# Four DiT-style layers on one core: preparing the keys of batch 2 between the row maxima of batch 0

## The reference

```python
q = (xq @ Wq + bq).reshape(B, Lq, nh, dh)
kv = (xkv @ Wkv + bkv).reshape(B, Lkv, 2, nh, dh)
scores = jnp.einsum('bqhd,bkhd->bhqk', q, k) / jnp.sqrt(jnp.float32(dh))
attn = jax.nn.softmax(scores, axis=-1)
out = jnp.einsum('bhqk,bkhd->bqhd', attn, v).reshape(B, Lq, H)
return x_q + (out @ Wp + bp)
```

## Time and profile before

| what | value |
|---|---|
| runs, us | 1910.01 (median), 1893.63, 1923.51 |
| profiled execution, us | 1909.95 |
| its span, us | 1908.1 |
| mean granted clock of PE | 0.893 of 2.4 GHz |
| PE busy | 1617.0 us, 85% of the span |
| DVE busy | 1151.9 us, 60% |
| ACT busy | 1002.8 us, 53% |
| POOL busy | 677.6 us, 36% |

### The profile page before, as it was taken

How to read it: one execution, slowest core, us unless ns; L and a number is a source line. 1 busy time by engine, 2 the same in 40 slices (tenths; PEclk the granted TensorE clock), 3 DMA queues, 4 the chain that set the end, 5 groups by cost and what they waited for, 6 DMA issues and landing times.

```text
span 1908.1 us, 54306 instructions
## 1 busy us (share of the span) xinstructions
PE 1617.0 (85%) x20495; PEld 1025.1 (54%) x20495; DVE 1151.9 (60%) x2289; ACT 1002.8 (53%) x1911; POOL 677.6 (36%) x899
## 2 busy tenths in 40 slices
PE   3788878599899998796699999987785899999986
PEld 3365544356566665343366666654342466666664
DVE  5354524377677775354577777771454776777752
ACT  1243423257677776142277777763242476777761
POOL 7000043436666644136166666510232122222200
PEclk9799989779999998697699999996796798999987
DMA  7022203244444432004345544430005444444310
GB/s 188 17 82 64 64 1 81 49 100 124 115 128 130 126 103 77 1 1 113 66 116 137 132 134 127 112 92 1 1 2 119 99 124 126 128 126 131 100 42 10
DMA packets 180074, 166.34 MB, mean 87 GB/s; under 512 B 69087, under 2 KB 169634, under 8 KB 179938
## 3 DMA queue, kind: packets, MB, share of 16 engines
q1 hardware_dynamic: 178354, 163.36, 33.3%
q10 hardware_dynamic: 1008, 1.05, 0.2%
q0 software_dynamic: 576, 0.02, 0.0%
HBM read 114.46 MB, written 40.08 MB: 81 GB/s over the span
## 4 chain that ended last, share of the span: by engine, by line
PE 63%; DVE 11%; ACT 10%; issue 7%; DMA 4%; SPq 3%; POOL 1%; ACTq 0%; DVEq 0%; POOLq 0%
PE PS L1155 11%; PE PS L1050 8%; PE PS L1181 7%; PE PS L1044 7%; PE PS L891 6%; PE PS L1129 5%; PE PS L1039 3%; PE PS L970 3%; SPq L426 2%; PE PS L1255 2%; DVE mx L1553 2%; ACT q_parts L824 2%; PE PS L988 2%; DMA k_dram<-k_lo 2%; ACT v_sb L758 2%
## 5 line engine op out<-in xcount | busy, mean ns | idle before, releaser
L1553 DVE TENSOR_REDUCE mx<-PS 112x1 f32<-112x500 f32 x1152 | 716.2, 673 | 246.9 <-PE PS L1129 242.4
L824 ACT ACTIVATE q_parts<-PS 125x448 f32<-125x448 f32 x1152 | 562.2, 544 | 111.9 <-PE PS L1181 108.4
L573 POOL CAST k_hi<-k_full 128x500 f16<-128x500 f32 x144 | 87.7, 609 | 645.5 <-issue 328.0
L608 POOL TENSOR_SCALAR cx<-cx,norm_b 125x128 f32<-125x128 f32 x384 | 304.8, 808 | 26.4 <-issue 19.3
L1129 PE MATMUL PS<-k_st,q_mx 50*112 50x500 f16 x1152 | 262.5, 403 | 45.4 <-issue 27.5
L1181 PEld LDWEIGHTS PS<-q_st,k_st 50*125 50x125 f16 x4608 | 185.5, 139 | 213.5 <-ACT q_parts L824 147.3
L1181 PE MATMUL PS<-q_st,k_st 50*125 50x112 f16 x4608 | 262.0, 235 | 40.1 <-ACT q_parts L824 22.8
L1155 PE MATMUL PS<-q_parts,v_sb 125*18 125x112 f32 x9216 | 292.8, 271 | 0.0
L1155 PEld LDWEIGHTS PS<-q_parts,v_sb 125*18 125x18 f32 x9216 | 219.4, 101 | 51.9 <-issue 43.8
L575 POOL TENSOR_TENSOR k_lo<-k_full,k_hi 128x500 f16<-128x500 f32 x144 | 164.1, 1139 | 21.1 <-POOL k_hi L573 3.5
L758 ACT ACTIVATE v_sb<-PS 125x512 f32<-125x512 f32 x144 | 87.0, 604 | 107.7 <-PE PS L1050 107.6
(11 more groups left out here) (267 smaller groups left out, 2090.9 us busy)
## 6 DMA issues: line engine op xcount, KB each, us to landing
k_st<-k_dram SPq DMA_DIRECT2D x864, 62.5 KB, 2.2
cx<-in_ctx SPq DMA_DIRECT2D x56, 672.0 KB
k_dram<-k_hi SPq DMA_DIRECT2D x144, 125.0 KB, 1.8
k_dram<-k_lo SPq DMA_DIRECT2D x144, 125.0 KB, 1.9
v_sb<-in_ctx SPq DMA_DIRECT2D x8, 672.0 KB
q_mx<-q_all SPq DMA_DIRECT2D x48, 99.8 KB
q_st<-q_all SPq DMA_DIRECT2D x48, 99.8 KB
cx<-in_ctx SPq DMA_DIRECT2D x56, 78.0 KB
```

What stands on the lines that cost most here:

```text
L608: last = pool.tensor_scalar(cx[:, p, c, :], cx[:, p, c, :], norm_b[:, p, 0, c:c + 1], norm_b[:, p, 1, c:c + 1], ALU.subtract, ALU.mult)
L824: act.activation(probs[:, c % RING, u * HR:(u + 1) * HR], PS[0:KC, (2 * c + u) % SC_RING, 0:HR], ACT.Exp).then_inc(sem("exp_done"), 1)
L1553: dve.tensor_reduce(mx[:, r, t:t + 1], PS[0:PW, MX_BANK + u % MX_RING, 0:TK], AX.X, ALU.max)\
```

## The change

In batch 0 alone of each cross layer, seven pieces of preparation move out of its attention into `first`. PE does V2 of batch 1 after unit 2 of the row maxima, T0, T1, T2 of batch 2 after units 5, 8, 11, and K0, K1, K2 after units 14, 17, 20. ACT does the copies in the same order, before it writes the shift rows of batch 0. V0 and V1 of batch 2 stay in steps 9 and 10 of the attention. GpSimd splits the keys of batch 2 at the end of `first`, now ahead of `normalise` of batch 3. SyncE issues the three `k_out` of batch 2 at the end of `first`, ahead of `q_scores(1)`, `q_max(2)` and `load(4)`. In the attention of batch 0 it only issues two `k_in`, and the third stays in the attention of batch 1. All other batches keep their order.

```diff
--- before.py
+++ after.py
@@ -57,6 +57,9 @@
 SLOT_MISC = {0: (True, 8), 1: (False, 0), 2: (False, 1), 3: (False, 2), 4: (False, 3), 6: (False, 4),
              8: (False, 5), 9: (False, 6), 10: (False, 7)}
 
+FIRST_MISC = {2: (1, 8), 5: (2, 0), 8: (2, 1), 11: (2, 2), 14: (2, 3), 17: (2, 4), 20: (2, 5)}
+FIRST_SLOT_MISC = {9: (False, 6), 10: (False, 7)}
+
 MAXES = [2, 2, 2, 2, 2, 2, 2, 3, 2, 3, 2, 0]
 JOIN_BANK = MX_BANK + 1
 PAIRS = B // 2
@@ -267,6 +270,9 @@
             for b in range(B - 4, B):
                 body(*[at(b + k) if b + k < B else None for k in range(4)])
 
+        def slot_misc(batch):
+            return FIRST_SLOT_MISC if isinstance(batch[0], int) and batch[0] == 0 else SLOT_MISC
+
         def ge_ahead(eng, *waits):
 
 
@@ -478,6 +484,8 @@
                     q_scores((0, 0, 0))
                     q_max((1, 0, 1))
                     stack_q(1, "q_stacked")
+                    for t in range(NT):
+                        k_out((2, 1, 0), t)
 
                 def attend(batch, following, behind, third):
                     b, i, p = batch
@@ -490,11 +498,15 @@
                         q_max(behind)
                         if not (isinstance(b, int) and b + 4 >= B):
                             load((b + 4, i + 2, p))
-                        k_out(behind, 0)
-                        k_in(behind, 0)
-                        k_out(behind, 1)
-                        k_in(behind, 1)
-                        k_out(behind, 2)
+                        if start:
+                            k_in(behind, 0)
+                            k_in(behind, 1)
+                        else:
+                            k_out(behind, 0)
+                            k_in(behind, 0)
+                            k_out(behind, 1)
+                            k_in(behind, 1)
+                            k_out(behind, 2)
 
                 pipeline(sp, first, attend)
 
@@ -623,7 +635,7 @@
                     if third and cr["norm"] is not None:
                         copies(third)
                         normalise(third)
-                    if behind:
+                    if behind and not (isinstance(batch[0], int) and batch[0] == 0):
                         for t in range(NT):
                             split_keys(layer, behind, t)
 
@@ -631,6 +643,8 @@
                     if cr["norm"] is not None:
                         copies((2, 1, 0))
                         normalise((2, 1, 0))
+                    for t in range(NT):
+                        split_keys(layer, (2, 1, 0), t)
 
                 pipeline(pool, first, attend)
 
@@ -813,9 +827,10 @@
 
                 def attend(batch, following, behind, _):
                     b, i, p = batch
+                    slots = slot_misc(batch)
                     for c in range(C):
                         n = C * (n0 + b) + c
-                        of_next, k = SLOT_MISC.get(c - 1, (False, None))
+                        of_next, k = slots.get(c - 1, (False, None))
                         if k is not None and (following if of_next else behind):
                             misc(following if of_next else behind, k)
                         ge(act, "pv_done", n - (RING - 1))
@@ -823,12 +838,15 @@
                             act.wait_ge(sem("scores_ready"), 2 * n + u + 1)
                             act.activation(probs[:, c % RING, u * HR:(u + 1) * HR],
                                            PS[0:KC, (2 * c + u) % SC_RING, 0:HR], ACT.Exp).then_inc(sem("exp_done"), 1)
-                    if C - 1 in SLOT_MISC and behind:
-                        misc(behind, SLOT_MISC[C - 1][1])
                     if following:
                         shift_rows(following)
 
-                pipeline(act, lambda: shift_rows((0, 0, 0)), attend)
+                def first():
+                    for b, k in FIRST_MISC.values():
+                        misc((b, b // 2, b % 2), k)
+                    shift_rows((0, 0, 0))
+
+                pipeline(act, first, attend)
 
             def self_attention(layer):
                 s = SELF[layer][0]
@@ -1187,6 +1205,9 @@
                 def first():
                     for u in range(UNITS):
                         unit((0, 0, 0), u)
+                        if u in FIRST_MISC:
+                            b, k = FIRST_MISC[u]
+                            misc((b, b // 2, b % 2), k)
                     shift((0, 0, 0))
 
                 def attend(batch, following, behind, _):
@@ -1205,8 +1226,8 @@
                         if c % 2 and c > 1:
                             for k in range(c - 3, c - 1):
                                 values(batch, k)
-                        if c in SLOT_MISC and c < C - 1:
-                            of_next, k = SLOT_MISC[c]
+                        if c in slot_misc(batch):
+                            of_next, k = slot_misc(batch)[c]
                             if following if of_next else behind:
                                 misc(following if of_next else behind, k)
                     if following:
```

## The result

The changed kernel took 1922.92 us (median of 4 runs, 1916.21 to 1941.13) beside 1901.82 us (4 runs, 1890.72 to 1923.51) for the kernel before. The ratio is 1.0172, with the interval 1.0125 to 1.0219; it takes the undisturbed executions alone, of which the 1923.51 of the kernel before, over 1.5% above its quickest, is not one, and the quotient of the two medians is 1.0111. So the kernel became slower, and whether by more or less than 2% the interval leaves open. The forecast of 1910.6 for 1909.95 us was a ratio of 1.0003. The measured 1922.92 us lies within the stated 1890 to 1927, but that range reaches to 1.009 times the kernel before, and the interval begins above it. The profiled execution took 1920.61 us, with a span of 1918.8 us and a mean granted clock of 0.884 (before 1908.1 and 0.893).

What follows compares the result with a forecast made beforehand. It took batch 0's attention as bound by PE and partly its clock, the stage ahead by DVE's row maxima. 1909.95 + 7.5 (first stages) - 0.8 (attentions) - 6.1 (stall) = 1910.6 us, range 1890 to 1927.

Steps and rivals of the forecast that it cites:

- first stage: Batch 0's 24 row maxima ahead of its attention: moved pieces add 2.5 us a layer, 7.5 us in all.
- attention of batch 0: Batch 0's attention in each cross layer: 24.6 us at a partly low PE clock, saving 0.8 us over three layers.
- stall in layer 3: Batch 4's attention in layer 3: PE's 2.32 us wait for k_st counted as gone, saving 6.1 us.
- turn of the loop in layer 1: Layer 1 at 488.73: an unexplained PE wait of 5.57 us, left as it is because the loop's instructions are the same.
- The moved queues: SyncE and GpSimd order: SyncE cost 0, at most 1 us if q_scores(1) were late; GpSimd has eight of twenty us spare.
- T and K ran between the maxima: Sign in the first stage of the profile after: transposes and K projections appear between row maxima from 381 on.
- no wait for k_st: Sign in layer 3 of the profile after: PE's wait of 2.32 us for k_st is gone.
- load(5): Sign in batch 1's attention: this SyncE load goes out at least 2 us earlier against the scores; 2.8 us worked out.
- Rival B: First stage stays at 1.2 GHz, K and V pieces of 2 us hold up the maxima: 1932 us, chance 0.15.
- Rival C: Stalls in the loops come, go or move, two of 6 us each: 1899 or 1923 us, chance 0.10.
- Rival D: Moved pieces in the first stage wait for their data until the attention, so nothing changes: 1910 us, chance 0.02.

Runs made afterwards that it cites:

- e2: Kernel before with only V2 of batch 1 moved into the first stage, T and K left in the attention, queues as before: 1906.20 us, ratio 1.0031.
- e3: Kernel before with V2 of batch 1 and T0 to T2 of batch 2 moved, K left in the attention, queues as before: 1907.26 us, ratio 1.0045.
- e1: Changed kernel with the SyncE key copies and GpSimd key split of batch 2 put back in the attention of batch 0: 1918.12 us, ratio 1.0109.
- e9: Changed kernel with ACT's wait for the query writes put behind the seven copies of the first stage: 1911.88 us, ratio 1.0051 to the kernel before.
- e14: Changed kernel, unchanged, profiled a second time: 1903.99 us in one run, attention of batch 0 in layer 3 at 23.4 us.
- e13: Changed kernel with eight added matmuls of 8 columns in the gap ahead of the shift of the first stage: 1949.60 us, ratio 1.0276 to the kernel before.
- e4: Changed kernel with one unused float32 128x500 matmul after steps 1, 2, 3, 4 and 6 of batch 0's attention: 1992.80 us, ratio 1.0507 to the kernel before.

## Why the prediction was wrong, step by step

**Step "first stage": mis-sized term.** It stood at 7.5 us in all with bounds 0 and 22.5, and measured 15.0 (14.1 in the second pair, 64.8 - 50.7). The mechanism is the one named, a piece and three matmuls longer than 1.77 us at 1.2 GHz. In layer 1 the six intervals of the chain are 13.00 us against 6 x 1.77 = 10.62: 2.4 us late, and the other 2.4 of the 4.8 us came before T0. I counted V late by 1.5 and 1.0 beside it for T and K together, as if the clock would rise at V. It rose at the second K. By layer, V costs 1.2 us (e2, 54.5 - 50.8 over three), the T 1.9 more (e3, 60.3 - 54.5) and the K 1.9 more (e1, 66.1 - 60.3): V was priced well, and T and K at a quarter of what they cost. I also passed over a wait: "ACT was idle" is true of its busy time, but ACT was waiting for the queries' DMA, and T0 stood 0.72 us behind the copy of V for it. e9 shows that this wait is worth little as long as the clock is low, and more once it is high.

**Step "attention of batch 0": right mechanism, wrong size.** This is the largest error, 10.1 us of the sum (-0.8 forecast, +9.3 measured, 83.9 - 74.6). In layer 1 the clock did stay at 1.2 GHz until V0 had run. Priced at 1.3 us for each of four pairs of steps, and at nothing for the first three steps, V0 and what follows, the attention came to 24.6 us; it took 28.8, 27.8 and 27.3. The price itself was good: 22.0 us at 0.84 is some 7 us at 1.2 GHz (2 x 0.16 x 22.0) for 2.6 us, 0.37 us each, where the line above has 0.32. What failed is how long it was charged. Four pairs are some 16 us, and the clocks of 0.53, 0.57 and 0.56 make 27, 24 and 24 us at 1.2 GHz; in layer 1 the row from 404 to 408 and that from 424 to 428, where V1 runs at 2.07 us, are both at 0.50. With 0.37 us for each of these us, 19.4 becomes 29.4, 28.2 and 28.3 us. Nor could my bound hold it: at the worst two more pairs a layer, 7 us lost in all. By the Trainium skill, page TensorE: Matmul & The Clock Gate, section "A second HAM failure mode: psum-queue depth-cycling", a PE that idles briefly and often would be throttled and warmed in turns. The trace of layer 1 shows no turns: 0.50 throughout from 404 to 428, and PE hardly idles there, 3.7 to 4.0 us of every 4 busy. Why the attention of e14's layer 3 came back to 2.4 GHz earlier and took 23.4 us, the runs do not tell.

**Step "stall in layer 3": counted, but not the kernel's.** The 6.1 us were indeed absent after (23.1 us in the row at 1610.50). But the second profile of the kernel before has only 24.2 - 23.1 = 1.1 us there. PE's waits for k_st in layer 3 are 2.9 us in the first profile of before and 0.5 in the second. One execution's wait went into the sum as if every run had it.

**Step "turn of the loop in layer 1": left as it is, and it changed.** Batches 3 and 4 took 27.9 + 26.2 us before and 22.5 + 23.5 after, 8.1 us less, and the wait of 5.57 us is gone. The second profile of before has it again, as 5.2 us, so it belongs to that kernel, and I had put its change at nothing. "The loop has the same instructions" was true and no reason, as e13 shows.

**What was right.** The moved queues show no cost (e1). T and K ran between the maxima from 381 on, and no wait for k_st was left in layer 3. load(5) went out at 437.59, 6.7 us after batch 1's first scores (430.9), for 430.26 - 420.9 = 9.4 before: 2.7 us earlier, where 2.8 were worked out. Rival B (1932 us) was the nearest in kind: K pieces of 2 us did hold up the maxima. It had the attention as wrong as the forecast, and its "no stall gone" is right if the stall was one execution's. Rival C's 1923 us meets the number by luck: it wanted two stalls more, and the two named ones were gone. Rival D fell.

**The sum by measurement.** First stages +15.0, attentions of batch 0 +9.3, the attentions of batches 1 to 14 of the three layers -10.9 (324.9 + 315.2 + 318.3 against 323.9 + 312.1 + 311.5), the rest of the span about -2.7: together +10.7, the difference of the spans. The timed ratio is larger, 24 to 42 us of 1901.82 by its interval; the difference of the medians, 21.1 us, is near the 21 to 24 us of the two stages. e1, whose loops are as short as those of after, measured 13 to 29 us against 19.9 in its stages. Why the changed kernel's four timed runs lost more than either pair of profiles shows stays open; a fifth run, e14, took 1903.99 us, 7.4 above the median of the kernel before beside it. Executions of the kernel before lie between 1884.81 and 1935.60 us, those of the changed one between 1903.99 and 1941.13, and in the profiles the parts that differ from one execution to the next are the clock of single stages (batch 14, 19.4 or 26.5 us) and, in e2 and e9, the loop of layer 1.

## What to carry to other kernels

Work that only fills PE can be worth more than its cover: before moving dense matmuls out of a stage, ask what will hold PE's clock there, and give what is left a second price, at 1.2 GHz for its whole length (here 27 to 29 us for 20 to 22). A stage with an idle PE at 1.2 GHz offers less room than its pieces at 2.4 GHz would need, so take the moved piece's time and the room at the same clock. And take no wait into a sum that a second profile of the same kernel doesn't show, nor trust a loop's time to stay when instructions ahead of it move.

## What the runs showed of the hardware that was not expected

Five added matmuls of 128 rows and 500 columns shortened a stage from 28.8 to 24.9 us (e4). PE busy for 3.7 to 4.0 of every 4 us, with matmuls of 50 rows and values with 18 columns of weights, stayed at 1.2 GHz for 24 us (after, layer 1), and the same work came back to 2.4 GHz by itself after some 12 us in e14's layer 3. In layer 1 of after the rises followed float32 pieces of 128 rows, the K (392 to 396) and V0 with V1 (428 to 432), though a lone V2 at 381 brought none; but three such K in a row stayed at 1.2 GHz in e9 (389.89 to 397.9), with PE busy all the time. In these profiles a rise came more often with such pieces (clock 0.79 to 0.86 in all attentions of e2, e3 and e4), and not always. Attentions of one loop took 22.5 and 23.5 us, or 30.0 and 26.7 with eight tiny matmuls added outside (e13), with single stalls of 8.2 us, and in e2 and e9 the loop was slow in an execution while others of the same kernel left no room for it.
